# Decoder block with top-8 routed experts: routed rows stored once and summed at the end, score masks by a rounded float32 product and by GpSimd's select, row stores dealt out over the schedule

## The reference, cut to what matters

```python
x = x + L0_attn(layernorm(x), ...)         # one causal head over a 32-wide compressed latent
x = x + L0_xattn(layernorm(x), ctx, mask)  # 32 heads of width 8 in 8 groups, keys from ctx
x = x + L0_ffn(layernorm(x), ...)          # 32 experts, inner width 96

# cross attention
scores = where(pad, -inf, scores); scores = where(causal, scores, -inf)
attn = softmax(scores)                     # per head, 128 x 128

# experts
top_vals, top_idx = top_k(softmax(x @ gate.T), 8)
renorm = top_vals / sum(top_vals); cum = cumsum(renorm)
num_keep = min(sum(cum < 0.8) + 1, 8)      # a token keeps its first num_keep experts
rw = kept values / their sum
out[token] = sum over kept e of rw[e] * (silu(g_e) * u_e) @ w_d[e].T
```

## Time and profile before

| what | value |
|---|---|
| time, median of 3 runs | 1075.66 us (1073.1 to 1075.86) |
| profiled execution, own time | 1084.95 us |
| its span | 1083.1 us |
| granted TensorE clock, mean | 0.82 of 2.4 GHz |
| busy share of the span | PE 63%, PEld 44%, POOL 41%, DVE 37%, ACT 32% |
| first stage | 0 to 554 us |
| second stage (first block load to last add landed) | 554 to 1029 us |
| third stage | 1029 to 1083 us |

### The profile page before, as it was taken

The page is one execution under the profiler, slowest core; times in us unless marked ns, Lnnn a source line. Parts: engine busy times, 40 slices in busy tenths (PEclk is TensorE's granted clock), DMA queues, the critical chain, the costliest instruction groups (busy, mean ns, idle before and its releaser), DMA issues.

```text
span 1083.1 us, 13176 instructions
## 1 busy us (share of the span) xinstructions
PE 684.6 (63%) x3277; PEld 476.1 (44%) x3277; DVE 397.3 (37%) x1588; ACT 348.8 (32%) x805; POOL 444.6 (41%) x501
## 2 busy tenths in 40 slices
PE   4876776777766776777545767565657575766500
PEld 2444433444434444444234656454546464655400
DVE  3355434554444455445323232222222232323222
ACT  3453345543345543345312222222222222322200
POOL 2123434333434323443326464545463645546500
PEclk9998889988889988889658787878787877878755
DMA  7513213431111111111136666666665656566566
GB/s 245 190 50 119 90 47 120 104 99 50 61 47 61 52 35 50 62 51 52 51 107 104 132 107 136 108 131 101 110 94 93 95 97 104 89 114 95 79 194 194
DMA packets 85738, 106.17 MB, mean 98 GB/s; under 512 B 10689, under 2 KB 79458, under 8 KB 85474
## 3 DMA queue, kind: packets, MB, share of 16 engines
q0 software_dynamic: 29184, 40.91, 21.8%
q1 hardware_dynamic: 56482, 64.41, 20.9%
HBM read 48.24 MB, written 57.04 MB: 97 GB/s over the span
## 4 chain that ended last, share of the span: by engine, by line
issue 30%; POOL 26%; PE 21%; DVE 11%; DMA 6%; ACT 3%; SPq 2%; POOLq 0%; DVEq 0%; ACTq 0%
POOL acc L380 14%; POOL rows L365 10%; PE bank L826 4%; PE bank L936 2%; PE bank L935 2%; PE bank L821 2%; DMA wgu_sb<-acc 2%; DVE NM L634 2%; ACT Q L388 2%; PE bank L954 1%; DVE wgu_sb L809 1%; DVE st_ln L540 1%; PE bank L955 1%; PE bank L944 1%; DMA xblk<-rows 1%
## 5 line engine op out<-in xcount | busy, mean ns | idle before, releaser
L380 POOL DMA_INDIRECT acc<-PT,xblk x96 | 149.1, 1553 | 147.1 <-ACT PT L388 122.6
L1036 PE MATMUL bank<-con,xblk 128*128 128x128 f32 x320 | 62.8, 330 | 169.6 <-DMA xblk<-rows 169.6
L1052 PE MATMUL bank<-wgu_sb,PT 128*128 (+1 forms) x640 | 167.7, 394 | 0.6 <-issue 0.5
L365 POOL DMA_INDIRECT rows<-rowb,idx x128 | 124.7, 974 | 70.7 <-issue 36.0
L388 ACT ACTIVATE PT<-bank 128x512 f32<-128x512 f32 x128 | 73.3, 595 | 225.1 <-PE bank L1036 192.0
L1052 PEld LDWEIGHTS bank<-wgu_sb,PT 128*128 128x128 f32 x640 | 126.8, 233 | 12.2 <-issue 10.6
L1036 PEld LDWEIGHTS bank<-con,xblk 128*128 128x128 f32 x320 | 47.1, 170 | 187.8 <-DMA xblk<-rows 168.0
L793 DVE COPY VC<-bank 96x256 f32<-96x256 f32 x80 | 33.7, 421 | 251.8 <-PE bank L1061 251.8
L634 DVE TENSOR_REDUCE NM<-bank 128x4 f32<-128x512 f32 x128 | 88.0, 689 | 42.0 <-PE bank L936 42.0
L1069 PE MATMUL bank<-wd_sb,VC 96*128 (+1 forms) x320 | 92.6, 415 | 0.5 <-DVE VC L793 0.5
L322 POOL TENSOR_TENSOR scalars<-mv_ln,scalars 128x1 f32<-128x1 f32 x48 | 9.6, 201 | 195.8 <-DVE mv_ln L542 195.8
(11 more groups left out here) (194 smaller groups left out, 1094.5 us busy)
## 6 DMA issues: line engine op xcount, KB each, us to landing
xblk<-rows SPq DMA_DIRECT2D x160, 144.5 KB, 2.5
wgu_sb<-acc SPq DMA_DIRECT2D x8, 1024.0 KB, 9.5
acc<-xTs SPq DMA_DIRECT2D x52, 128.0 KB, 1.9
wgu_sb<-wgu_d SPq DMA_DIRECT2D x8, 768.0 KB, 5.1
rows<-pad SPq DMA_DIRECT2D x33, 152.0 KB, 2.1
wd_sb<-wd_d SPq DMA_DIRECT2D x2, 1536.0 KB, 9.8
xin<-x_d SPq DMA_DIRECT2D x16, 128.0 KB, 2.3
ctx_sb<-ctxT_d SPq DMA_DIRECT2D x16, 128.0 KB, 2.3
```

Of the source, the lines that this page charges most:

```text
L365: gp.indirect_dma_start(out=rows, out_offset=bass.IndirectOffsetOnAxis(ap=idx[b % 2][:, k:k + 1], axis=0), in_=rowb[b % 2][:, :], in_offse ...
L380: gp.indirect_dma_start(out=acc[a], out_offset=bass.IndirectOffsetOnAxis(ap=xblk[q % FEED][:, j, D + NE:ROW].bitcast(i32), axis=0), in_=yb ...
L1036: last = t.transpose(XT_PS[q % 2][:, j * D + k * P:j * D + (k + 1) * P], xblk[q % FEED][:, j, k * P:(k + 1) * P], ident)
L1052: last = t.matmul(GU_PS[q % 2][:, j * 2 * NI:(j + 1) * 2 * NI], xTb[q % 2][:, j, k * P:(k + 1) * P], wgu_sb[:, k, one_of(expert[i]), :].sq ...
```

## The change

- The expert output of each routed slot is no longer added into an accumulator. Each (token, k) has its own row in a new DRAM tensor `parts` of 2048 x 8 rows. GpSimd's store is a plain indirect store with a bounds check; padding slots carry an index past the end and are left out. No store waits for an earlier one at its address.
- To know k, the row also carries the token's eight slot positions (`ROW` grows from 289 to 297 floats of the 304). VectorE's `meta` compares them with the slot's own position (`mine`), gets k, and adds it to 8 x token: `dst[q % FEED]`. Before it writes `dst` it waits for the stores of pair q - FEED.
- `FEED` goes from 5 to 4. SP's load of pair q waits for `dst` of pair q - FEED in place of the landed adds.
- The zero stores, the stores of `x2` and `x1b` go; `x2` stays in SBUF for all 16 batches.
- The third stage reads `parts` (16 loads of 1 MB, five buffers), VectorE sums over k with a reduction whose inner step is one row of 256 floats, adds `x2`, and SP stores each batch.
- `nident`, the causal mask and `maskn` become fp32r; before they were bf16.
- The causal mask product of the transposed scores is gone. GpSimd zeroes the masked entries of `PT` with `affine_select` (128 x 512) after each exponential, and `pv` waits for that (`pm`).
- The eight row stores of a batch become eight steps `sc0` to `sc7`, 2.2 time units apart in `ORDER`.
- Some tiles share memory, and some semaphores are merged.

```diff
-ROW = D + NE + 1
+ROW = D + NE + TOP + 1
-NACC = 4
-FEED = 5
+FEED = 4
...
-      ... "po": 49.4, "sc": 50.5}
+      ... "po": 49.4, **{f"sc{k}": 50.5 + 2.2 * k for k in range(TOP)}}
...
-        acc = [nc.dram_tensor(f"acc{a}", (NTOK + P, D), f32, kind="Internal").ap() for a in range(NACC)]
+        parts = nc.dram_tensor("parts", (NTOK * TOP, D), f32, kind="Internal").ap()
-        nident16, causal16, causT16 = (sb(n, [P, P], bf16) for n in ("nident16", "causal16", "causT16"))
+        nident, causalr = (sb(n, [P, P], f32r) for n in ("nident", "causalr"))
-        maskn, padcol = sb("maskn", [P, NB * P], bf16), sb("padcol", [P, NB])
+        maskn, padcol = sb("maskn", [P, NB * P], f32r), sb("padcol", [P, NB])
...
+        def stored(eng, q):
+            eng.wait_ge(S["pr"][q % FEED], 32 * (q // FEED + 1))
...
@@ SP
-                if b == 1:
-                    for a in range(1, NACC):
-                        for t in range(NB + 1):
-                            sp.dma_start(acc[a][t * P:(t + 1) * P, :], xTs[1][:, :]).then_inc(S["z0"], 16)
-                    sp.dma_start(acc[0][NTOK:, :], xTs[1][:, :]).then_inc(S["z0"], 16)
...
-                sp.dma_start(acc[0][b * P:(b + 1) * P, :], x2[b % 2][:, :]).then_inc(S["x2st"][b % 2], 16)
...
-                    added(sp, q - FEED)
+                    sp.wait_ge(S["dst"], nth("dst", q - FEED))
...
+            for q in range(NPAIR - FEED, NPAIR):
+                stored(sp, q)
+            sp.wait_ge(S["Y"], nth("Y", NPAIR - 1))
+            for b in range(NB):
+                if b >= NFIN:
+                    sp.wait_ge(S["fsum"], nth("fsum", b - NFIN))
+                sp.dma_start(fin[b % NFIN], parts[b * P * TOP:(b + 1) * P * TOP, :].rearrange("(p k) d -> p (k d)", k=TOP)).then_inc(S["fin"][b % NFIN], 16)
+                if b >= 3:
+                    store(b - 3)
@@ GpSimd
+            def s_(g):
+                def f(b):
+                    pool.wait_ge(S["e"], nth("e", b, g + 1))
+                    gp.affine_select(out=PT[:, g, :, :], in_=PT[:, g, :, :], compare_op=ALU.is_ge, fill=0.0, base=0,
+                                     pattern=[[0, HG], [1, P]], channel_multiplier=-1).then_inc(S["pm"], 1)
+                return f
...
             for q in range(NPAIR):
                 pool.wait_ge(S["yc"], nth("yc", q))
-                pool.wait_ge(S["bl"][q % FEED], 32 * (q // FEED + 1))
+                pool.wait_ge(S["dst"], nth("dst", q))
                 for j in range(2):
-                    if turn > 0:
-                        pool.wait_ge(S["ac"][a], 16 * turn)
-                    gp.indirect_dma_start(out=acc[a], ..., in_=yb[q % FEED][:, j, :], in_offset=None, compute_op=ALU.add)
+                    gp.indirect_dma_start(out=parts, out_offset=bass.IndirectOffsetOnAxis(ap=dst[q % FEED][:, j:j + 1], axis=0),
+                                          in_=yb[q % FEED][:, j, :], in_offset=None, bounds_check=NTOK * TOP - 1, oob_is_err=False).then_inc(S["pr"][q % FEED], 16)
@@ ScalarE, yc
-                    added(act, q - FEED)
+                    stored(act, q - FEED)
@@ VectorE, meta
+                for j in range(2):
+                    i = 2 * q + j
+                    last = v.scalar_tensor_tensor(kjnk[:, 2 * (q % 2) + j, :], xblk[q % FEED][:, j, D + NE:D + NE + TOP], mine[:, i:i + 1], iota_k, ALU.is_equal, ALU.mult,
+                                                  accum_out=ksl[q % 2][:, j:j + 1])
+                last.then_inc(S["k"], 1)
+                dve.wait_ge(S["k"], nth("k", q))
+                if q >= FEED:
+                    stored(dve, q - FEED)
+                v.tensor_tensor(dst[q % FEED][:, :], ksl[q % 2][:, :], xblk[q % FEED][:, :, ROW - 1], ALU.add).then_inc(S["dst"], 1)
@@ VectorE, third stage
+            for b in range(NB):
+                v.tensor_reduce(total[b % 4], fin[b % NFIN].rearrange("p (k d) -> p d k", k=TOP), AX, ALU.add).then_inc(S["fsum"], 1)
+                v.tensor_tensor(total[b % 4], total[b % 4], x2[:, b, :], ALU.add).then_inc(S["fadd"], 1)
@@ TensorE
-                    t.matmul(o[:, :].rearrange("p (g m) -> p g m", g=HG), nident16[:, :], maskn[...]...)
+                    t.matmul(o[:, :].rearrange("p (g m) -> p g m", g=HG), nident[:, :], maskn[...]...)
...
-                    t.matmul(o[:, :], KA[b % 2][:, g, :], Q2[...], start=True, stop=False)
-                    t.matmul(o[:, :].rearrange("p (h n) -> p h n", h=HG), nident16[:, :], causT16[:, :].unsqueeze(1).to_broadcast([P, HG, P]),
-                             start=False, stop=True).then_inc(S["s"], 1)
+                    t.matmul(o[:, :], KA[b % 2][:, g, :], Q2[...], start=True, stop=True).then_inc(S["s"], 1)
...
-                    pe.wait_ge(S["e"], nth("e", b, 4 * n + 4))
+                    pe.wait_ge(S["pm"], nth("pm", b, 4 * n + 4))
```

More of the change, by code:

```diff
@@ L38 @@
       "g1": 45.0, "g2": 45.8, "g3": 46.1, "g4": 46.4, "g5": 46.7, "g6": 47.0, "g7": 47.3, "g8": 47.6, "g9": 47.9, "g10": 48.2,
[1 row of a table removed]
+      "g11": 48.5, "g12": 48.8, "g13": 49.1, "rk": 47.2, "po": 49.4, **{f"sc{k}": 50.5 + 2.2 * k for k in range(TOP)}}
 W_AT = {f"w{n}": 25.0 + 12.0 * n for n in range(10)}
@@ L153, in shared @@
             return [flat[:, at:at + n] for at in (next(room) for _ in range(2))]
+        kjnk, ksl, dst = sb("kjnk", [P, 4, TOP]), two("ksl", [P, 2]), [sb(f"dst{n}", [P, 2], i32) for n in range(FEED)]
         wjnk, wsl = sb("wjnk", [P, 4, NE]), two("wsl", [P, 2])
@@ L237, in ldc @@
                     small("w_bias", (bo_sb[:, :], bo))
-                    small("w_con", (cob[:, :], con2), (tok_sb[:, :], tokid))
+                    small("w_con", (cob[:, :], con2))
             def w(n):
@@ L250, in n3, with store @@
             def n3(b):
-                sp.wait_ge(S["x2"], nth("x2", b))
                 if b == 1:
-                    sp.wait_ge(S["pad"], 4)
+                    sp.wait_ge(S["pad"], 3)
                     sp.dma_start(rows[NE * REG * P:, :], pad[:, :]).then_inc(S["dummy"], 16)
-                sp.dma_start(acc[0][b * P:(b + 1) * P, :], x2[b % 2][:, :]).then_inc(S["x2st"][b % 2], 16)
+            def store(b):
+                sp.wait_ge(S["fadd"], nth("fadd", b))
+                sp.dma_start(out[b], total[b % 4]).then_inc(S["out"][b % 4], 16)
             schedule({"ldx": ldx, "ldc": ldc, "n3": n3, **{f"w{n}": w(n) for n in range(10)}})
@@ L815, in _ @@
             for k in range(KC):
-                last = t.matmul(V_PS[:, k * DC:(k + 1) * DC], l_tokv[:, k * P:(k + 1) * P], l_comp[:, :], start=True, stop=True)
+                last = t.matmul(V_PS[:, k * DC:(k + 1) * DC], l_tokv[:, k * P:(k + 1) * P], l_comp, start=True, stop=True)
             last.then_inc(S["setup_p"], 1)
```

203 lines of the change are left out of this document (93 added, 110 removed), and 9 rows, old and new, of tables (AT, names).

## The result

The kernel after takes 927.65 us (923.1 to 930.2, four runs), the kernel before 1075.76 us in the same group of runs: ratio 0.861, 95% interval 0.855 to 0.867. It is faster, but by 148 us where 261 us was forecast, and 43 us above the upper end of the range. The profiled execution has a span of 928.4 us.

A forecast was written before the change was run, and what follows sets the result against it. The prediction took waits that close a circle, with no engine full, to bound both long stages. Experts -205, batches -60 and third stage +6 from 1083.1 gave an 824 us span, 815 us predicted, range 765 to 885.

The forecast's parts named there:

- The circle of the experts: Experts: loads waiting for landed adds cost 5.8 us a pair; without that wait 3.1 to 3.3, stage 270 us, gain 205.
- The shorter circle through `dst`: Experts: VectorE's `meta` waits for stores of q-3; 2.3 to 2.9 us a pair, under PE's 3.04, so slack remains.
- Rival 3: Experts stay in a circle, PE idles and falls to 1.2 GHz: 910 us, far end 1020; chance 0.10.
- The padding phase: Experts, the 32 pairs with padding stores: SP's third issue makes 3.1 to 3.3 us a pair; 3.3 taken.
- The block of row stores: Batches: eight stores on the chain dealt out; base period without the block 26.1 us, against 32.1.
- The mask product and the selects: Batches: eight products leaving PE save 1.8 us a batch, selects on POOL add 3.5; period 27.8 us, gain 60.
- Rival 1: Experts: checked store costs POOL the adding store's 1.55 us, POOL becomes the bound: 857 us; chance 0.14.
- rival 4: Batches: the select is a slow loop and POOL the bound; at 5 us a select 1224 us; chance 0.03.
- Rival 2: Batches: selects and VectorE hold each other up, 3.2 us a period, 45 us in all: 860 us; chance 0.12.
- fp32r: Mask product in fp32r: streaming unchanged, a wider weight load of at most 0.5 us for the eight.
- The third stage: End of kernel: 59 to 60 us against 54, loss 6, bounds -4 and +25; reduction at 2.3 us.
- The sum: Whole kernel: 1083.1 - 205 - 60 + 6 = 824 us span, predicted time 815 us; forecast's chance 0.60.

The follow-up runs named there:

- h1: The kernel after, unchanged, run for the third time: 887.4 us, ratio 0.813.
- f4: e7 with nident and the masks in bf16 instead of fp32r: 852.7 us, ratio 0.789.
- e7: The kernel after with the mask product instead of selects, halving adds in the third stage, padding stores on ScalarE's queue: 792.0 us, ratio 0.734.
- e8: The kernel after with each batch's eight row stores moved so none stands between POOL's selects: ratio 0.817, and 0.854 when run again.

## Why the prediction was wrong, step by step

**The circle of the experts** was right. The loads left it, PE became the bound, 3.01 us a pair against 3.1 forecast, and in h1 the stage took 274.9 us against 270. The shorter circle through `dst` shows (in h1 VectorE waited 0.76 us for a landed store at 750.53, and PE 0.36 us behind it) and costs next to nothing, as forecast: it is all that PE stood in the 100 us from 700.

**What failed there** is that no term and no rival had signals of PE arriving late: 41 us in the groups that have them, 274.9 to 315.7. Rival 3 had an experts stage that stays too long, but by its cause, the circle, and with a clock at 1.2 GHz; the clock was 1.00 and 0.93 in the two stretches above. The cause stays open. The trace of the kernel before gives no hint of them: none of PE's signals in its experts is recorded more than 0.15 us behind its product.

**The padding phase** was mis-sized: 3.58 us a pair where 3.3 was taken, 9 us in 32 pairs. SP's rate of 2.1 us for two loads plus a third issue gave 3.1 to 3.3. In the result's run a round of SP took 3.5 to 3.9 us (its loads start at 600.12, 604.05, 607.92 and 611.41 us), and in h1 3.4 to 3.9, with 1.4 to 2.2 us for the two loads alone. 4 us came back from the later pairs.

**The block of row stores** was right. The period without it, mask product in place, is 26.55 us where 26.1 was taken.

**The mask product and the selects** are the step that failed in the batches. The select was priced at 1.0 us and took 0.63; by the prediction's own bounds a select of 0.52 us gave a period of 25.5 us, and it was 30.7. The late `pv0` was seen, its wait sized at 2.0 us against 1.3 measured; `pv1`, put 2.7 us late, waited for no select but in the last batch. What was left out is that PE's clock falls there, by the wait or by the products that are gone, which no run separates: `pv` and `wq` took 2.6 us a batch more, the scores and transposes 2.2, waits included. Of the two terms, the products' -1.8 us was right (1.9 measured), and the selects' +3.5 us was +6.1; the net is +4.15 us in place of +1.7, though the select itself took a third less than its price. The earlier trace rows showed a clock of 0.88 in the batches; the prediction had no term for its fall to 0.82.

**Rival 1** (a checked store at 1.55 us) and **rival 4** (a slow select) fell with 980 and 634 ns. **Rival 2** fell too: the selects took 624 to 805 ns, median 634, beside whatever VectorE did.

**fp32r** cost nothing, as said (f4). **The third stage** lost 16.3 us where 6 was taken; the step that failed is the reduction at the rate of a dense add, 2.3 us against 3.58. Its bound of +25 held it.

**The sum.** Of the 113 us, 48 are the batches (2.9 us in each of 14 periods, and a last batch that takes 8 us longer from its residual to the end, 67.5 us against 59.4 before, where e7's takes 57.9), 41 the late signals, 5 the padding phase net of the faster pairs, 10 the strided reduction, 7 the offset between profile and median, and 2 rounding. Without the late signals the kernel is at 887 us (h1), 2 us above the range and 72 above the forecast; most of that is the selects and the reduction.

## What to carry to other kernels

An operation moved off TensorE to save its time can cost more than it saves if TensorE then waits for the other engine: price the wait, and the work behind it at 1.2 GHz instead of 2.4 (here 1.3 us of waits a batch, and 2.6 us more in the `pv` and `wq` behind them). A reduction that steps from plane to plane need not run at the rate of a dense add; here the sum over eight planes was faster as halving adds of contiguous planes. When a stage whose code an edit doesn't touch moves by 40 us, run both kernels again side by side before giving the edit the credit: here e8 seemed to gain 0.044 of the ratio, and side by side the two stood level (0.850 and 0.854).

## What the runs showed of the hardware beyond that

Signals of PE can reach ScalarE and VectorE 1.3 to 2.4 us after the recorded end of the product, several at once, at a granted clock of 1.00, in some groups of runs and not in others, for the same program (experts 275 us, and 314 to 318 us). Of the groups whose chip is on record no two ran on the same one, so the chip and the occasion aren't told apart, and the same traces lack semaphore records, so an effect of the recording isn't ruled out. An indirect store of 128 rows of 1 KB keeps POOL 0.98 us with a bounds check, the same as without one, and successive ones start 1.28 us apart. POOL's select over 128x512 fp32 in place takes 0.63 us. An fp32r identity product over 512 columns takes as long as the bf16 one (397 and 390 ns, period 26.55 us in both).
